# An adaptive FFN kernel on one Trainium2 core: the head's weight spread, load order and one low-part split moved

## What is computed

```python
# x (64, 32, 512), cond (64, 128)
h = gelu(cond @ W0 + b0); h = gelu(h @ W1 + b1)            # 128 wide, exact gelu
att = softmax(h @ W2 + b2)                                  # (64, 8)
agg_w = einsum('bk,koi->boi', att, weight)                  # 8 kernels of 32x32
agg_b = att @ bias_k
y = einsum('boi,bih->boh', agg_w, x) + agg_b[:, :, None]
up = relu(y @ up_w) ** 2                                    # 512 -> 1024
shared = up @ down_w                                        # 1024 -> 512
scale = sum(top2(y @ gate_w))                               # per token
routed = (((y @ fc1_w) @ expert_w) * scale) @ fc2_w
out = x + layernorm(shared + routed) * gamma + beta
```

## Time and profile before

| | before |
|---|---|
| median of 3 runs | 256.34 us (256.32 to 256.38) |
| the profiled execution | 256.47 us |
| its span | 254.7 us |
| TensorE busy (matmul) | 247.9 us, 97% |
| VectorE, ScalarE, GpSimd busy | 157.5, 80.8, 36.5 us |
| bytes by DMA | 15.59 MB, 61 GB/s |
| granted TensorE clock over the span | 1.00 |

### The profile page before, as it was taken

How to read it: one execution, slowest core, us unless ns; L and a number is a source line. 1 busy time by engine, 2 the same in 40 slices (tenths; PEclk the granted TensorE clock), 3 DMA queues, 4 the chain that set the end, 5 groups by cost and what they waited for, 6 DMA issues and landing times.

```text
span 254.7 us, 3495 instructions
## 1 busy us (share of the span) xinstructions
PE 247.9 (97%) x1291; PEld 207.2 (81%) x1291; DVE 157.5 (62%) x274; ACT 80.8 (32%) x137; POOL 36.5 (14%) x34
## 2 busy tenths in 40 slices
PE   8999999999999999999999999999999999999992
PEld 7778887988888888888888888888888888788891
DVE  3789999944448974644447985464444953406453
ACT  4389746411003452321112534331111355202100
POOL 1400010000117110001114410001111700001110
PEclk9999999999999999999999999999999999999999
DMA  6994713001111400001111210000011100000111
GB/s 164 335 320 159 299 39 129 0 0 44 41 41 41 167 0 0 3 0 42 41 41 41 96 69 0 0 0 8 33 41 44 41 0 0 3 0 9 74 44 41
DMA packets 10443, 15.59 MB, mean 61 GB/s; under 512 B 1088, under 2 KB 4928, under 8 KB 10432
## 3 DMA queue, kind: packets, MB, share of 16 engines
q1 hardware_dynamic: 9984, 15.33, 17.4%
q10 hardware_dynamic: 448, 0.11, 0.2%
HBM read 11.23 MB, written 4.20 MB: 61 GB/s over the span
## 4 chain that ended last, share of the span: by engine, by line
PE 90%; DMA 2%; issue 2%; DVE 2%; SPq 1%; POOL 0%; POOLq 0%; ACT 0%; DVEq 0%
PE ps L922 27%; PE ps L924 27%; PE ps L923 27%; PE ps L893 4%; DMA experts_sb<-in_experts_dram 2%; PE ps L988 2%; PE ps L850 1%; PE ps L946 1%; PE ps L940 1%; PE ps L942 1%; PE ps L899 1%; DVE up_lo L615 1%; DVE h_full L632 1%; SPq L322 0%; POOL rstd L410 0%
## 5 line engine op out<-in xcount | busy, mean ns | idle before, releaser
L923 PE MATMUL ps<-down_lo,sq_hi 128*128 128x512 f32 (+1 forms) x136 | 51.3, 377 | 0.0
L924 PE MATMUL ps<-down_hi,sq_lo 128*128 128x512 f32 (+1 forms) x136 | 51.2, 377 | 0.0
L922 PE MATMUL ps<-down_hi,sq_hi 128*128 128x512 f32 (+1 forms) x136 | 51.2, 377 | 0.0
L922 PE MATMUL ps<-h_hi,up_hi 128*128 128x512 f32 x120 | 46.7, 389 | 0.0
L924 PE MATMUL ps<-h_hi,up_lo 128*128 128x512 f32 x120 | 46.7, 389 | 0.0
L923 PE MATMUL ps<-h_lo,up_hi 128*128 128x512 f32 x120 | 46.7, 389 | 0.0
L410 POOL TENSOR_TENSOR rstd<-mv,half 128x1 f32<-128x1 f32 x16 | 15.3, 956 | 162.2 <-DVE mv L710 157.2
L500 ACT ACTIVATE relu_sq<-ps 128x512 f32<-128x512 f32 x32 | 19.1, 597 | 58.2 <-PE ps L924 45.7
L703 DVE TENSOR_TENSOR y_buf<-ps,y_buf 128x512 f32<-128x512 f32 x15 | 10.4, 692 | 41.0 <-PE ps L924 40.7
L676 DVE CAST sq_hi<-relu_sq 128x512 fp32r<-128x512 f32 x32 | 23.9, 748 | 14.4 <-ACT relu_sq L502 13.8
L922 PEld LDWEIGHTS ps<-down_hi,sq_hi 128*128 128x128 f32 x136 | 25.6, 188 | 4.7
(11 more groups left out here) (135 smaller groups left out, 304.5 us busy)
## 6 DMA issues: line engine op xcount, KB each, us to landing
out_dram<-late SPq DMA_DIRECT2D x15, 256.0 KB, 2.0
x_cur<-in_x_dram SPq DMA_DIRECT2D x3, 1024.0 KB, 5.2
late<-in_down_w_dram SPq DMA_DIRECT2D x4, 512.0 KB, 5.3
late<-in_up_w_dram SPq DMA_DIRECT2D x3, 512.0 KB, 9.5
x_cur<-in_x_dram SPq DMA_DIRECT2D x2, 512.0 KB, 7.5
experts_sb<-in_experts_dram SPq DMA_DIRECT2D x3, 256.0 KB, 4.0
agg_b<-aggb_dram SPq DMA_DIRECT2D x1, 768.0 KB, 4.7
latents_sb<-in_latents_dram SPq DMA_DIRECT2D x1, 528.0 KB, 4.8
```

The source lines that it names most:

```text
L922: nc.tensor.matmul(dst, a_hi, b_hi, start=first, stop=False)
L923: nc.tensor.matmul(dst, a_hi, b_lo, start=False, stop=False)
L924: return nc.tensor.matmul(dst, a_lo, b_hi, start=False, stop=last)
```

## The change

Five edits, all in the head.

1. The transposed kernels: VectorE transposes them four times, each time into another group of 32 partitions, and GpSimd copies them into `weight_T`. The product with `repeat`, its memory and clearings, and VectorE's copy are gone.
2. The hidden layers run on 64 columns. Idle products: 8, 2, 2 in place of 9 and 4.
3. Loads: the first expert loads go ahead of b2; on ScalarE's queue the second part of `mlp_sb` goes first, and `bias_sb` after the first gelu; the latents' load goes ahead of the bias rows' store.
4. The bias rows' product and their copy are made ahead of the first mix tiles and of the copy of `att_P`.
5. Low part of up chunk 1: by GpSimd, with a semaphore of its own (`up_lo1_ready`). ScalarE splits chunks 0 and 1 ahead of the first high part of h. TensorE takes the two high products of a piece first, then the low product of chunk 0, then that of chunk 1.

```diff
-        H1 = ps[:, 4, 0:2 * NB].rearrange("p (a b) -> p a b", a=2)
-        H2 = ps[:, 4, 2 * NB:4 * NB].rearrange("p (a b) -> p a b", a=2)
+        H1 = ps[:, 4, 0:NB]
+        H2 = ps[:, 4, NB:2 * NB]
...
         def _(sp):
             sp.dma_start(mlp_sb[:, 0:NB + D], mlp[:, 0:NB + D]).then_inc(mlp_loaded[0], 16)
+            for m in range(LC):
+                sp.dma_start(experts_sb[:, m, FIRST], experts_v[:, m, FIRST]).then_inc(experts_loaded[m], 16)
             sp.dma_start(b2_rows[:, :], kernels[0, C * C + C:C * C + C + K].partition_broadcast(NB)
                          ).then_inc(b2_loaded, 16)
-            for m in range(LC):
-                sp.dma_start(experts_sb[:, m, FIRST], experts_v[:, m, FIRST]).then_inc(experts_loaded[m], 16)
             sp.dma_start(experts_sb[:, :, REST], experts_v[:, :, REST]).then_inc(experts_loaded[LC], 16)
...
+            sp.dma_start(latents_sb[:, :, :], latents_v).then_inc(latents_loaded, 16)
             sp.wait_ge(rows_copied, 1)
             sp.dma_start(aggb_dram.rearrange("(b o) -> b o", o=C), aggb_rows[:, :]).then_inc(rows_stored, 16)
-            sp.dma_start(latents_sb[:, :, :], latents_v).then_inc(latents_loaded, 16)
...
         def _(pool):
...
+            pool.wait_ge(weight_t_ready, G)
+            nc.gpsimd.tensor_copy(weight_T[:, :, :], weight_t.rearrange("p (k o) -> p o k", o=C)
+                                  ).then_inc(weightT_copied, 1)
             pool.wait_ge(bias_loaded, 16)
...
+            second = slice(P, 2 * P)
+            pool.wait_ge(up_hi_ready, 2)
+            nc.gpsimd.tensor_tensor(up_lo[:, :, second], up_raw[:, :, second], up_hi[:, :, second].bitcast(fp32),
+                                    ALU.subtract).then_inc(up_lo1_ready, 1)
...
         def _(act):
...
+            act.dma_start(mlp_sb[:, NB + D:], mlp[:, NB + D:]).then_inc(mlp_loaded[1], 16)
             act.dma_start(weight_raw[:, :, :], weight_v).then_inc(weight_loaded, 16)
-            act.dma_start(mlp_sb[:, NB + D:], mlp[:, NB + D:]).then_inc(mlp_loaded[1], 16)
-            act.dma_start(bias_sb[:, :], kernels[0:K2, C * C:]).then_inc(bias_loaded, 16)
...
+            act.dma_start(bias_sb[:, :], kernels[0:K2, C * C:]).then_inc(bias_loaded, 16)
             act.wait_ge(h2_done, 1)
...
         def _(dve):
...
-            nc.vector.transpose(weight_t[:, :, :].rearrange("i k o -> i (k o)"),
-                                weight_raw[:, :, :].rearrange("o k i -> o (k i)")).then_inc(weight_t_ready, 1)
+            for g in range(G):
+                nc.vector.transpose(weight_t[g * C:(g + 1) * C, :],
+                                    weight_raw[:, :, :].rearrange("o k i -> o (k i)")).then_inc(weight_t_ready, 1)
...
-            dve.wait_ge(weightT_done, 1)
-            nc.vector.tensor_copy(weight_T[:, :, :], WEIGHT_T.rearrange("p (k o) -> p o k", o=C)
-                                  ).then_inc(weightT_copied, 1)
...
             first_mix_bias(1)
-            split_up(1)
             first_mix_low(0)
...
         def _(pe):
...
-            pe.wait_ge(weight_t_ready, 1)
-            nc.tensor.matmul(WEIGHT_T, repeat[:, :, :].rearrange("j g i -> j (g i)"), weight_pad,
-                             start=True, stop=True).then_inc(weightT_done, 1)
+            nc.tensor.matmul(H2, w1_sb, hid1[:, :], start=True, stop=True).then_inc(h2_done, 1)
+            stay_warm(2)
...
                     for m in (0, 1):
                         cols = slice(m * P, (m + 1) * P)
-                        pe.wait_ge(up_lo_ready, m + 1)
+                        pe.wait_ge(up_hi_ready, m + 1)
                         nc.tensor.matmul(ps[:, UP_BANK[m], :], up_hi[:, c, cols], h_hi[:, c, :],
                                          start=(c == 0), stop=False)
-                        nc.tensor.matmul(ps[:, UP_BANK[m], :], up_lo[:, c, cols], h_hi[:, c, :],
-                                         start=False, stop=False)
+                    pe.wait_ge(up_lo_ready, 1)
+                    nc.tensor.matmul(ps[:, UP_BANK[0], :], up_lo[:, c, 0:P], h_hi[:, c, :],
+                                     start=False, stop=False)
+                    pe.wait_ge(up_lo1_ready, 1)
+                    nc.tensor.matmul(ps[:, UP_BANK[1], :], up_lo[:, c, P:2 * P], h_hi[:, c, :],
+                                     start=False, stop=False)
```

More of the change, by code:

```diff
@@ L265, in adaln_ffn_kernel @@
         up_lo_ready = sem("up_lo_ready")
+        up_lo1_ready = sem("up_lo1_ready")
         fc1_hi_ready = sem("fc1_hi_ready")
@@ L336, in _ @@
             sp.wait_ge(up_hi_ready, IC)
-            sp.wait_ge(up_lo_ready, IC)
+            sp.wait_ge(up_lo_ready, IC - 1)
+            sp.wait_ge(up_lo1_ready, 1)
             for i in range(4):
@@ L434, in _ @@
             act.wait_ge(h1_done, 1)
-            nc.scalar.activation(hid1[:, :], H1[:, 0, :], ACT.Gelu, bias=b0_sb).then_inc(gelu_done, 1)
+            nc.scalar.activation(hid1[:, :], H1, ACT.Gelu, bias=b0_sb).then_inc(gelu_done, 1)
+            act.dma_start(bias_sb[:, :], kernels[0:K2, C * C:]).then_inc(bias_loaded, 16)
             act.wait_ge(h2_done, 1)
-            nc.scalar.activation(hid2[:, :], H2[:, 0, :], ACT.Gelu, bias=b1_sb).then_inc(gelu_done, 1)
+            nc.scalar.activation(hid2[:, :], H2, ACT.Gelu, bias=b1_sb).then_inc(gelu_done, 1)
             act.wait_ge(warmed, 1)
@@ L477, in _ @@
             bias_high(1)
+            act.wait_ge(rows_done, 1)
+            nc.scalar.copy(aggb_rows[:, :], AGGB_ROWS).then_inc(rows_copied, 1)
             act.wait_ge(first_terms_ready, 2)
@@ L482, in _ @@
             split_up(0)
-            act.wait_ge(rows_done, 1)
-            nc.scalar.copy(aggb_rows[:, :], AGGB_ROWS).then_inc(rows_copied, 1)
+            split_up(1)
             first_mix_high(0)
-            split_up(1)
             first_mix_high(1)
@@ L853, in _ @@
             pe.wait_ge(dve_const, 1)
-            stay_warm(9)
+            stay_warm(8)
             pe.wait_ge(const_ready, 1)
             pe.wait_ge(mlp_loaded[0], 16)
-            nc.tensor.matmul(H1, w0_sb, cond_T.unsqueeze(1).to_broadcast([D, 2, NB]),
-                             start=True, stop=True).then_inc(h1_done, 1)
-            stay_warm(4)
+            nc.tensor.matmul(H1, w0_sb, cond_T, start=True, stop=True).then_inc(h1_done, 1)
+            stay_warm(2)
             pe.wait_ge(dve_const, 3)
             pe.wait_ge(sel_ready, 1)
-            pe.wait_ge(padded, 4)
-            pe.wait_ge(repeat_ready, 1)
+            pe.wait_ge(padded, 2)
             pe.wait_ge(mlp_loaded[1], 16)
             pe.wait_ge(gelu_done, 1)
-            nc.tensor.matmul(H2, w1_sb, hid1[:, :].unsqueeze(1).to_broadcast([D, 2, NB]),
-                             start=True, stop=True).then_inc(h2_done, 1)
-            pe.wait_ge(weight_t_ready, 1)
-            nc.tensor.matmul(WEIGHT_T, repeat[:, :, :].rearrange("j g i -> j (g i)"), weight_pad,
-                             start=True, stop=True).then_inc(weightT_done, 1)
+            nc.tensor.matmul(H2, w1_sb, hid1[:, :], start=True, stop=True).then_inc(h2_done, 1)
+            stay_warm(2)
             pe.wait_ge(gelu_done, 2)
@@ L890, in _ @@
             fold_expert(1, 1, 1).then_inc(q_done, 1)
+            pe.wait_ge(bias_loaded, 16)
+            pe.wait_ge(attT_copied, 1)
+            nc.tensor.matmul(AGGB_ROWS, att_T[0:K, :], bias_raw[0:K, :], start=True, stop=True).then_inc(rows_done, 1)
             def mix_chunk(b, c, bank):
@@ L913, in _ @@
             first_mix_tiles(0, (2, 3)).then_inc(mix_done, 1)
-            pe.wait_ge(bias_loaded, 16)
-            nc.tensor.matmul(AGGB_ROWS, att_T[0:K, :], bias_raw[0:K, :], start=True, stop=True).then_inc(rows_done, 1)
             for c in range(1, HC):
```

15 lines of the change are left out of this document (2 added, 13 removed).

## The result

| | before | after |
|---|---|---|
| median | 256.39 us (256.32 to 256.61, 8 runs) | 257.52 us (257.00 to 258.18, 8 runs) |
| ratio, 95% interval | 1 | 1.0044 (1.0028 to 1.0059) |
| the profiled execution | 256.47 us, span 254.7 | 258.18 us, span 256.4 |

The change is slower by 0.44%, 1.1 us, where 256.2 was forecast and 256.8 was the end of the range. The runs are also spread over 1.2 us, four of them at 257.0 to 257.3 and four at 257.7 to 258.2; before, all eight lay within 0.3. The profiled execution is the slowest of the eight, so it shows the loss in full: its span is 1.7 longer.

What follows compares the result with a forecast made beforehand. TensorE was taken to bound the kernel (90% of the chain), so head edits count only by moving its dense stretch: first h_lo product at 16.44 plus 4.66 gives 21.10 against 21.23, -0.13 from 256.34, so 256.2 us; range 255.4 to 256.8.

Steps and rivals of the forecast that it cites:

- part 1: Layers, kernels' spread, idle products: logits start near 5.2, gain mostly unused because b2 lands at 6.1; transposes free.
- The sum: Mark, first product of up chunk 2, moves from 21.23 to 21.10: -0.13, giving 256.2 us.
- terms at about 8.4: Softmax chain in the head stays where it was within 0.1, its terms at about 8.4 against 8.47.
- the clock rival: TensorE stays longer at its lower clock, first folds up to 2.1 longer: 256.8 us, or 258.9 with second folds; chance 0.06.
- Half of it covered: With slow first folds, terms, mix and tiles come about 1.1 later, but half of that is covered: 256.8 us.
- They end by 5.3, before b2: VectorE's four kernel transposes end by 5.3, before b2 lands, so the logit addition behind them isn't delayed.
- Part 2: Order of loads: first expert loads issued 0.6 earlier, the rest gains 0.3 (0 to 0.6), second folds start at 8.8.
- Part 3: TensorE up to the first up product: bias product at 12.1, TensorE free for up products at 14.8 to 14.9, against 15.08.
- ScalarE's new order costs nothing: ScalarE splits chunk 1 before the first h_hi, which still ends at 14.8, when TensorE is ready.
- Part 4: Chunk 1's subtraction on GpSimd takes 1.28 and holds VectorE; first h_lo product starts at 16.44 in place of 16.57.
- the fast rival: GpSimd and VectorE don't hold each other at the up split: mark 0.8 earlier, 255.5 us; chance 0.31 shared with larger load gain.
- about -0.4: Lower end of the total, with the loads gaining 0.6 and GpSimd's subtraction taking 1.04.

Runs made afterwards that it cites:

- e9_gap_only: Kernel before with idle products 8 and 2 in place of 9 and 4, layers still on 128 columns: 258.23 us, ratio 1.0043, 8 of 12 runs late.
- e1_fill: The change with idle products 10, 4, 4 in place of 8, 2, 2: 256.69 us, ratio 1.0023, 2 of 12 runs late.
- e12_best: The change with all head loads as before, bias rows' product back in its place, idle products 9, 4, 4: 256.66 us, ratio 1.0019, 4 of 12 late.
- e10_narrow_only: Kernel before with the layers on 64 columns, idle products kept at 9 and 4: 256.38 us, ratio 1.0006, 2 of 12 runs late.
- e3_fill_b2: The change with idle products 10, 4, 4 and b2 loaded ahead of the first expert loads again: 256.67 us, 2 of 12 runs late.
- e5_loads_fill: The change with ScalarE's three loads as before and idle products 9, 4, 4: 256.60 us, ratio 1.0039, 4 of 11 runs late.
- e11_experts_first: Kernel before with only the first expert loads moved ahead of b2: 256.72 us, ratio 1.0034, 3 of 12 runs late.
- e8_part5: Kernel before with the fifth edit alone (up chunk 1's low part on GpSimd, with its new orders): 256.37 us, ratio 1.0003.
- e2_fill_dve: The change with idle products 10, 4, 4 and chunk 1's low-part subtraction back on VectorE: 256.95 us, ratio 1.0027, 3 of 12 runs late.
- e6_loads_wide: The change with ScalarE's three loads as before, layers on 128 columns, idle products 9, 4, 3: 256.56 us, ratio 1.0008, 2 of 12 late.
- e4_before_gaps: Kernel before with layers on 64 columns and idle products 8 and 2: 257.43 us, ratio 1.0049.

## Why the prediction was wrong, by its own steps

**The step that failed is in part 1.** The sum booked the idle products that were taken out as a gain (0.07) and left the first folds at the upper level, with "terms at about 8.4". Measured: the first folds took 3.78 in place of 1.99 and the terms started at 10.21. That term, at nothing in the sum, stood only as the clock rival. The prediction gave the rival its place (two gaps of 0.4, the first folds at the lower level), its mechanism (folds end near 9, terms about 1.1 later), 256.8 as its time, and a chance of 0.06. It is what happened: folds till 9.7, terms 1.74 later. Fewer idle products alone do it (e9_gap_only, 8 of 12 runs 2 us late), and more of them make it rarer (e1_fill, 0.8 faster with 2 late of 12). The prediction gives no reason for the small chance; it says itself that TensorE was busy "without a break before that rise". The trace of before could not say whether less would do; it showed only the case without a hole. That was a reason for an open chance, not for a small one.

**Its price was too low too.** "Half of it covered" was wrong. The first folds' end is 1.6 later (9.68 against 8.05). For the terms nothing covers it, because the spread of the attention weights stands behind the folds on TensorE, and the mix and GpSimd's bias rows hang on the terms' side. On TensorE itself the wait for the experts' rest (0.58 before) is gone and takes up 0.4: the second folds start 1.21 later. In e9_gap_only the two groups of runs are about 2.1 apart.

**Part 1, the rest.** The logits at 5.20 in e12_best look like the 5.2 forecast, but that is luck: there the clock was up from 4.3 on. At the lower level the halved layers gave 0.16 and not 0.4 (e10_narrow_only), and in the change itself the logits came at 5.58. The transposes were not free. They took 1.83, near the 1.72 estimated, but were forecast at 3.5 and started at 4.49, behind a load of 3.3. "They end by 5.3, before b2" had the order wrong: b2 was early (5.7, forecast 6.1), and the transposes, ending at 6.32, were the later of the two. In this run both are hidden by the slow folds. GpSimd's copy took 0.61 against 0.8.

**Part 2.** The experts' rest landed at 7.7, better than the 8.8 taken and than the end of the bounds. The term that was missing is what the same edit takes from others. The kernels' load went from 2.3 to 3.3, and with b2 first again it took 2.2 (e3_fill_b2); where ScalarE's loads were put back, the layers' second part went to 3.4 (e5_loads_fill). `bias_sb` went from 2.7 to 5.4: it took 3.5 with the expert loads first and its early issue (e5_loads_fill), so most of this is its own move behind the first gelu. Only b2 had been followed. The order of the expert loads alone costs 0.3 (e11_experts_first).

**Part 3.** From the bias product to the first up product 2.91 after, 2.89 before; 2.7 was forecast (14.8 less 12.1). "ScalarE's new order costs nothing" was wrong: TensorE waited 0.20 for the first h_hi, which stood behind chunk 1's high part on ScalarE.

**Part 4 was right by its steps, but one row under it was misread.** Forecast 1.28 for GpSimd, measured 1.35 and 1.28; the first h_lo "about 1.3", measured 1.17 and 1.35; from the bias product to the first h_lo product 4.34 forecast, 4.17 measured, 4.38 in e8_part5 and before. Alone it changes nothing (e8_part5). The rule of the Trainium skill (SBUF — State Buffer, section SBUF: two separate sides), that such a pair excludes each other for the whole instruction, is borne out: in e8_part5 VectorE's subtraction ended 0.54 after GpSimd's, next to the 0.55 read from the earlier trace rows. The prediction saw one exception, the subtraction at 35.90, as "two in 1.47". The row says x1: it is one subtraction of 1.47 where the others take 0.69, and it ended at 37.37, 0.55 after GpSimd's product (35.78 + 1.04). So both places of the earlier trace rows agree with the rule, and the fast rival ("as at 35.78"), which shared a chance of 0.31, rested on that misreading. The lower end of the sum doesn't come out of its terms either: the sum's -0.13, 0.3 more from the loads and 0.24 less for GpSimd give -0.67, not "about -0.4".

**The clock by the skill.** The traces show the folds' passes 0.45 apart in one execution and 0.23 in the other, at the same place. The Trainium skill (TensorE: Matmul & The Clock Gate, section Part 1: The HAM clock gate) says that the default state is the throttled one and that activity releases it; by that rule idle products are work that counts, and the run without three of them (e9_gap_only) agrees. e1_fill and e2_fill_dve, with the same work and the clock up from 6.3 and from 10.1, show that the work of TensorE in this kernel doesn't settle it alone.

**Open.** What decides between the two outcomes of the same work isn't shown. Whether halved layers make late runs likelier by themselves was not told apart (2 of 12 in both e10_narrow_only and e6_loads_wide, with different holes; 1 of 122 before). No late run of e12_best was profiled. The four runs of the change at 257.0 to 257.3 were not profiled either; that their clock rose a little earlier is argued from e4_before_gaps (folds of 3.02, time 257.42), not shown.

## What to carry to other kernels

Products that only keep TensorE busy are part of the critical path's timing: whoever shortens or removes real work among them should fill the place, and must look at many runs, because the loss comes in some runs and not in others. A median over three runs of e9_gap_only could have said 256.1 or 258.3. When a large load is issued earlier, follow every small load that is in flight at that time, on all queues, to the instruction that waits for it and to what is queued behind that. A rival that the profile can't price deserves the chance that one's ignorance has, not a small one.

## What was not expected of the hardware

- In 16 profiled executions TensorE's upper level began anywhere from 4.3 to 11.0 us after the start, and the time goes with it: 255.9 to 256.7 where it began by 6.3, 258.2 to 258.5 where it began at 9.9 or later.
- The profile's column of the granted clock reads 1.00 also for the time ahead of the first record of the clock, in which the folds' passes were 0.43 apart and not 0.22. At the start of a program the spacing of matmuls has to be read instead.
- Three idle products fewer in the first 5 us, a hole of 0.3, made 8 of 12 runs late and left four untouched: the same program has times 2.1 us apart. But a hole of 0.7 went with an early rise (e5_loads_fill), and a stream with no hole above 0.1 with a late rise (e2_fill_dve).
- A 2.5 KB load took 5.4 to 5.7 us to land when it was issued near 4 us, behind the large loads of the other queue (after, e1_fill, e3_fill_b2), and 2.7 when it was issued at 1.69 (before).
